# A two-layer spectral filter on one core: the last task's inverse rows are loaded step by step, and its neighbour's held groups go through three pairs of banks

## The reference

```python
f = jnp.fft.fft2(xf, axes=(1, 2), norm='ortho')          # layer 0
Xk = (f.real - f.imag)[:, :, :Wf].reshape(..., 8, 48)[:, lo:hi, :kept]   # kept = 23
o1 = relu(einsum('bhwni,nio->bhwno', Xk, w1[0]) + b1[0])
o2 = einsum('bhwno,nio->bhwno', o1, w2[0]) + b2[0]
x = jnp.fft.ifft2(softshrink(o2, 0.01), s=(H, W), axes=(1, 2), norm='ortho').real + x

xf = jnp.fft.rfft2(x, axes=(1, 2), norm='ortho')         # layer 1, complex weights
o1r, o1i = relu(xr*w1[0] - xi*w1[1] + b1[0]), relu(xi*w1[0] + xr*w1[1] + b1[1])
o2r, o2i = softshrink(o1r*w2[0] - o1i*w2[1] + b2[0]), softshrink(o1i*w2[0] + o1r*w2[1] + b2[1])
y = jnp.fft.irfft2(o2r + 1j*o2i, s=(H, W), axes=(1, 2), norm='ortho') + x
```

## Time and profile before

| what | value |
|---|---|
| median of three runs | 519.68 us |
| the profiled execution: its own time | 517.78 us |
| the profiled execution: its span | 516.0 us |
| mean granted TensorE clock | 0.975 |
| TensorE busy (products) | 479.6 us, 93% |
| VectorE, ScalarE, GpSimd busy | 308.1, 209.8, 172.5 us |
| moved by DMA | 105.25 MB, mean 204 GB/s |

### The profile page before, as it was taken

The page is one execution under the profiler, slowest core; times in us unless marked ns, Lnnn a source line. Parts: engine busy times, 40 slices in busy tenths (PEclk is TensorE's granted clock), DMA queues, the critical chain, the costliest instruction groups (busy, mean ns, idle before and its releaser), DMA issues.

```text
span 516.0 us, 14920 instructions
## 1 busy us (share of the span) xinstructions
PE 479.6 (93%) x6172; PEld 342.5 (66%) x6172; DVE 308.1 (60%) x674; ACT 209.8 (41%) x473; POOL 172.5 (33%) x194
## 2 busy tenths in 40 slices
PE   4679999999999999999999999999999999999763
PEld 1357787777777677767777677767777767886521
DVE  7634456457754677456764677456763577567643
ACT  0015544553355443543354433554345434444201
POOL 9821323123441244223442144312433122322134
PEclk9959999999999999999999999999999999999978
DMA  9998773677899688886989588987989665644498
GB/s 213 265 237 236 213 187 110 145 207 182 252 233 243 165 201 264 218 216 178 267 224 252 152 210 263 228 204 187 256 213 258 169 168 163 148 108 113 121 224 268
DMA packets 77416, 105.25 MB, mean 204 GB/s; under 512 B 7744, under 2 KB 63826, under 8 KB 77350
## 3 DMA queue, kind: packets, MB, share of 16 engines
q1 hardware_dynamic: 57766, 56.74, 41.4%
q0 software_dynamic: 10608, 40.66, 29.8%
q10 hardware_dynamic: 8976, 6.90, 5.7%
HBM read 52.84 MB, written 51.43 MB: 202 GB/s over the span
## 4 chain that ended last, share of the span: by engine, by line
PE 77%; DMA 7%; DVE 5%; POOL 3%; issue 2%; ACT 2%; SPq 1%; ACTq 1%; POOLq 0%
PE ps L702 13%; PE ps L636 13%; PE ps L727 12%; PE ps L689 11%; PE ps L597 10%; PE ps L649 8%; PE ps L714 5%; PE ps L665 4%; PE ps L675 3%; DMA img<-x 2%; DVE img L572 2%; DMA wt<-weights 2%; POOL xs L392 2%; DVE ns L546 2%; ACT p L463 1%
## 5 line engine op out<-in xcount | busy, mean ns | idle before, releaser
L572 DVE TENSOR_TENSOR img<-ps,img 90x768 f32<-90x768 f32 x92 | 82.6, 900 | 19.0 <-PE ps L636 15.5
L392 POOL TENSOR_TENSOR xs<-xs,nt 128x360 f32<-128x360 f32 (+1 forms) x48 | 41.6, 866 | 147.9 <-DVE nt L524 122.5
L636 PE MATMUL ps<-jr,cst 64*90 64x384 f32 (+1 forms) x358 | 80.0, 515 | 6.4 <-DVE img L572 5.7
L597 PE MATMUL ps<-img,cst 128*64 128x384 f32 (+1 forms) x368 | 70.1, 494 | 8.9 <-DMA img<-x 8.0
L401 POOL DMA_DIRECT2D y<-img x42 | 34.7, 826 | 130.7 <-DVE img L572 130.3
L456 ACT ACTIVATE o<-ps,wt 97x180 f32<-97x180 f32 (+1 forms) x96 | 33.9, 406 | 108.7 <-PE ps L689 108.7
L546 DVE SCALAR_TENSOR_TENSOR ns<-p,ps 109x384 f32<-109x384 f32 x96 | 53.1, 553 | 38.2 <-ACT p L463 33.4
L702 PE MATMUL ps<-wt,o 128*64 128x96 f32 x1472 | 74.4, 250 | 0.1
L649 PEld LDWEIGHTS ps<-cst,bt 128*64 128x64 f32 x1472 | 62.5, 140 | 16.9 <-issue 13.9
L702 PEld LDWEIGHTS ps<-wt,o 128*64 128x64 f32 x1472 | 65.4, 138 | 12.5 <-issue 12.5
L689 PE MATMUL ps<-xs,wt 64*97 64x180 f32 (+1 forms) x768 | 68.9, 317 | 3.4 <-POOL xs L392 3.2
(11 more groups left out here) (43 smaller groups left out, 410.9 us busy)
## 6 DMA issues: line engine op xcount, KB each, us to landing
y<-img POOLq DMA_DIRECT2D x35, 540.0 KB, 5.4
img<-x POOLq DMA_DIRECT2D x25, 540.0 KB, 8.6
scr_i<-et SPq DMA_DIRECT2D x48, 270.0 KB, 5.4
scr_f<-fs SPq DMA_DIRECT2D x154, 72.0 KB, 3.4
bt<-scr_f SPq DMA_DIRECT2D x40, 270.0 KB, 5.5
jr<-scr_i SPq DMA_DIRECT2D x48, 216.0 KB, 5.3
img<-x ACTq DMA_DIRECT2D x10, 576.0 KB, 7.8
y<-img SPq DMA_DIRECT2D x11, 270.0 KB, 3.7
```

Of the source, the lines that this page charges most:

```text
L392: nc.gpsimd.tensor_tensor(re, re, nt[s % 2][:, :, 0:kws(s), 0:H], ALU.subtract).then_inc(re_ok, 1)
L572: nc.vector.tensor_tensor(y, p, y, ALU.add).then_inc(i_add, 1)
L597: last = mm(ps[64 * r:64 * r + 64, P3 + g % 2, 0:(b - a) * HC], K["w_fwd"], img[t % IMGS][:, a:b, :].rearrange("p h c -> p (h c)"), start= ...
L636: last = mm(ps[0:W, B0 + r, 0:n], K["w_inv"][64 * r:64 * r + 64, :], set_rows(t, j)[64 * r:64 * r + 64, at, 0:n], start=True, stop=True)
```

## The change

Four things are changed together, all of them at the end of the list.

1. The rows for task 7's inverse W are no longer loaded in five sets after the last step, but step by step in the tile `f0`, which task 0's forward W used: behind the store of step i (from i = 1 on), SP waits until step i - 1 is stored and loads its eight rows for all 12 groups (`last_rows`, three DMAs). The rows of the last step follow in the entry ("last_rows",): SP loads the first half of each group and the last group, ACT's queue the second half. Task 7's first product waits for all of them.
2. The five held groups of task 6, g7 to g11 (`HELD` = 7), go through the pairs P2, P1, P3, P2, P1 (`pair_of`) and not all through P3.
3. POOL's stores of task 6's image rows behind g7, g9 and g11 wait until task 7's rows have all landed.
4. `LAST_POOL` has three groups and not four; ACT copies them in turn into `p1` and a free `et` tile, and issues their stores at its end. VectorE adds the other nine.

The products of task 7 read 48 rows of `f0` and not 64 of `jr` (the 16 others were zero).

```diff
@@ -24,11 +24,12 @@
...
 GROUPS = -(-H // 4)
+HELD = 7
 XCH = 8
...
 WARM = 7
-LAST_POOL = (1, 4, 7, 10)
+LAST_POOL = (1, 4, 7)
 JSETS = [(0, 3), (3, 6), (6, 9), (9, 11), (11, 12)]
...
@@ -149,7 +150,7 @@
...
     order += held
-    order += [("rows", TASKS - 1, j) for j in range(len(JSETS))]
+    order.append(("last_rows",))
     order += [("inv", TASKS - 1, g) for g in range(GROUPS)]
...
@@ -220,7 +221,8 @@
...
         j_ld = [sem(f"j{k}_loaded") for k in range(JR)]
-        j_tail = [sem(f"last_set{j}_loaded") for j in range(JR, len(JSETS))]
+        l_ld = [sem(f"last_rows{k}_loaded") for k in range(2)]
+        y_last_act = sem("y_of_last_task_stored_act")
         i_mm, i_add = sem("inv_product"), sem("inv_added")
...
@@ -241,11 +243,22 @@
...
-        def set_rows(t, j):
-
-            if t == TASKS - 1 and j >= JR:
-                return bt[j - JR][:, 0:(JSETS[j][1] - JSETS[j][0]) * 2 * HC].rearrange("p (g c) -> p g c", c=2 * HC)
-            return jr[bank_of(t, j)[0]]
+        def last_rows(i, r):
+            k0, k1 = 2 * STEP * i, min(2 * STEP * (i + 1), 2 * KWP)
+            rows = scr_i[TASKS - 1].rearrange("k e h c -> (k e) h c")[k0:k1]
+            four = rows[:, 0:H - 1, :].rearrange("q (g r s) c -> q g r (s c)", r=2, s=2)[:, :, r, :]
+            return four, f0[64 * r + k0:64 * r + k1, 0:GROUPS - 1, :], rows[:, H - 1, :], f0[k0:k1, GROUPS - 1, 0:HC]
+        def held_no(t, g):
+            return g - HELD if t == TASKS - 2 else -1
+        def pair_of(t, g):
+            if t == TASKS - 1:
+                return (P0, P1, P2, P3)[g % 4]
+            return (P2, P1, P3)[held_no(t, g) % 3] if held_no(t, g) >= 0 else P3
...
@@ -325,33 +338,41 @@
...
                                  et[s % 2][0:2 * H, :, :]).then_inc(e_st[s % 2], 16)
+                    if t == TASKS - 1 and i > 0:
+                        sp.wait_ge(e_st[(s - 1) % 2], 16 * ((s - 1) // 2 + 1))
+                        for r in range(2):
+                            four, to, one, to_one = last_rows(i - 1, r)
+                            sp.dma_start(to, four).then_inc(l_ld[0], 16)
+                        sp.dma_start(to_one, one).then_inc(l_ld[0], 16)
                 if kind == "rows" or (kind == "inv" and what[0] < TASKS - 1 and what[1] in (2, 5)):
...
                     k, used = bank_of(t, j)
-                    landed = j_tail[j - JR] if t == TASKS - 1 and j >= JR else j_ld[k]
                     if j == 0:
...
                         sp.wait_ge(j_clr, j + 1)
-                    if t == TASKS - 1 and j >= JR:
-                        sp.wait_ge(a_mm, 2 * NT)
-                    elif used:
+                    else:
                         m = t * len(JSETS) + j - JR
...
                     if g0 == GROUPS - 1:
-                        sp.dma_start(set_rows(t, j)[0:2 * KWP, 0, 0:HC], rows[:, 4 * g0, :]).then_inc(landed, 16)
+                        sp.dma_start(jr[k][0:2 * KWP, 0, 0:HC], rows[:, 4 * g0, :]).then_inc(j_ld[k], 16)
                     else:
...
                         for r in range(2):
-                            sp.dma_start(set_rows(t, j)[64 * r:64 * r + 2 * KWP, 0:g1 - g0, :], four[:, :, r, :]).then_inc(landed, 16)
-                if kind == "inv" and what[0] == TASKS - 1:
+                            sp.dma_start(jr[k][64 * r:64 * r + 2 * KWP, 0:g1 - g0, :], four[:, :, r, :]).then_inc(j_ld[k], 16)
+                if kind == "last_rows":
+                    sp.wait_ge(e_st[(NT - 1) % 2], 16 * ((NT - 1) // 2 + 1))
+                    four, to, one, to_one = last_rows(STEPS - 1, 0)
+                    sp.dma_start(to, four).then_inc(l_ld[0], 16)
+                    sp.dma_start(to_one, one).then_inc(l_ld[0], 16)
+                if kind == "inv" and what[0] == TASKS - 1 and what[1] not in LAST_POOL:
                     g, (h0, h1), (b, f) = what[1], hrows(what[1]), divmod(TASKS - 1, HALVES)
...
                     sp.dma_start(out[b, h0:h1, :, f * HC:(f + 1) * HC].rearrange("h w c -> w h c"), img[(TASKS - 1) % IMGS][0:W, h0:h1, :]).then_inc(y_last, 16)
-            sp.wait_ge(y_last, 16 * GROUPS)
+            sp.wait_ge(y_last, 16 * (GROUPS - len(LAST_POOL)))
...
@@ -398,6 +419,10 @@
...
                     pool.wait_ge(i_add, t * GROUPS + g + 1)
+                    if t == TASKS - 2 and g >= HELD:
+                        pool.wait_ge(l_ld[0], 16 * (3 * (STEPS - 1) + 2))
+                        pool.wait_ge(l_ld[1], 16)
                     pool.dma_start(out[b, r0:r1, :, f * HC:(f + 1) * HC].rearrange("h w c -> w h c"), img[k][0:W, r0:r1, :]).then_inc(y_st[k][c], 16)
...
@@ -406,7 +431,8 @@
...
                     y = img[t % IMGS][0:W, h0:h1, :].rearrange("p (r s) c -> p r (s c)", r=2)
-                    nc.gpsimd.tensor_tensor(y, p1[0:W], y, ALU.add).then_inc(i_pool, 1)
+                    p = (p1[0:W], et[NT % 2][0:W].rearrange("p (r s) c -> p r (s c)", r=2))[n % 2]
+                    nc.gpsimd.tensor_tensor(y, p, y, ALU.add).then_inc(i_pool, 1)
                 if kind == "load" and what[0] % STEPS == 3 and what[0] // STEPS >= 2:
...
@@ -467,14 +493,26 @@
...
                     nc.scalar.activation(et[s % 2][0:2 * H, 0::2, :], ps[0:2 * H, P0, 0:2 * HC].rearrange("p (k c) -> p k c", c=HC), ACT.Copy).then_inc(e_act, 1)
+                if kind == "last_rows":
+                    act.wait_ge(e_st[(NT - 1) % 2], 16 * ((NT - 1) // 2 + 1))
+                    four, to, _, _ = last_rows(STEPS - 1, 1)
+                    act.dma_start(to, four).then_inc(l_ld[1], 16)
                 if kind == "inv" and what[0] == TASKS - 1 and what[1] in LAST_POOL:
                     t, g = what
-                    n, B0 = LAST_POOL.index(g), 2 * (g % 4)
+                    n, B0 = LAST_POOL.index(g), pair_of(t, g)
                     act.wait_ge(i_mm, t * GROUPS + g + 1)
                     act.wait_ge(d1_ss, 2 * NT)
-                    if n > 0:
-                        act.wait_ge(i_pool, n)
-                    nc.scalar.activation(p1[0:W], ps[0:W, B0:B0 + 2, 0:2 * HC], ACT.Copy).then_inc(i_act, 1)
+                    act.wait_ge(e_st[NT % 2], 16 * ((NT - 2) // 2 + 1))
+                    if n > 1:
+                        act.wait_ge(i_pool, n - 1)
+                    p = (p1[0:W], et[NT % 2][0:W].rearrange("p (r s) c -> p r (s c)", r=2))[n % 2]
+                    nc.scalar.activation(p, ps[0:W, B0:B0 + 2, 0:2 * HC], ACT.Copy).then_inc(i_act, 1)
+            b, f = divmod(TASKS - 1, HALVES)
+            for n, g in enumerate(LAST_POOL):
+                h0, h1 = hrows(g)
+                act.wait_ge(i_pool, n + 1)
+                act.dma_start(out[b, h0:h1, :, f * HC:(f + 1) * HC].rearrange("h w c -> w h c"), img[(TASKS - 1) % IMGS][0:W, h0:h1, :]).then_inc(y_last_act, 16)
+            act.wait_ge(y_last_act, 16 * len(LAST_POOL))
...
@@ -562,7 +600,7 @@
...
                     h0, h1 = hrows(g)
-                    B0 = P3 if t < TASKS - 1 else 2 * (g % 4)
+                    B0 = pair_of(t, g)
                     dve.wait_ge(i_mm, t * GROUPS + g + 1)
...
@@ -606,34 +644,40 @@
...
                     t, g = what
-                    j = jset[g]
-                    k, _ = bank_of(t, j)
-                    if g == JSETS[j][0]:
-                        if t == TASKS - 1 and j >= JR:
-                            pe.wait_ge(j_tail[j - JR], 16 * set_dmas(j))
-                        else:
-                            pe.wait_ge(j_ld[k], rows_landed(t, j))
-                    at = g - JSETS[j][0]
-                    if t < TASKS - 1:
-                        B0 = P3
-                        vacate(0)
-                        vacate(1)
-                    else:
-                        B0 = 2 * (g % 4)
-                        if g < 4:
-                            pe.wait_ge(i_add, t * GROUPS)
-                            pe.wait_ge(t_add, 2 * NT)
-                            pe.wait_ge(d0_ss, 2 * NT)
+                    B0, n = pair_of(t, g), held_no(t, g)
+                    if t == TASKS - 1:
+                        if g == 0:
+                            pe.wait_ge(l_ld[0], 16 * (3 * (STEPS - 1) + 2))
+                            pe.wait_ge(l_ld[1], 16)
                             pe.wait_ge(e_act, NT)
                             pe.wait_ge(e_dve, NT)
+                        elif g < 4:
+                            users = [m for m in range(HELD, GROUPS) if pair_of(TASKS - 2, m) == B0]
+                            pe.wait_ge(i_add, (TASKS - 2) * GROUPS + (users[-1] if users else HELD - 1) + 1)
                         elif g - 4 in LAST_POOL:
...
                             pe.wait_ge(*last_added(g - 4))
+                    else:
+                        j = jset[g]
+                        k, _ = bank_of(t, j)
+                        if g == JSETS[j][0]:
+                            pe.wait_ge(j_ld[k], rows_landed(t, j))
+                        if n == 0:
+                            pe.wait_ge(d1_ss, 2 * NT)
+                        elif n == 1:
```

(10 more changed lines are left out.)

## The result

The changed kernel takes 522.36 us (median of 20 runs, 519.11 to 527.69), the kernel before beside it 518.74 (20 runs, 516.10 to 520.44). The ratio is 1.0075, 95% interval 1.0054 to 1.0095: slower by 0.75%, where 516.5 us, within 513.0 to 518.8, and a gain had been forecast. The profiled execution took 523.22 us with a span of 521.4, for 517.78 and 516.0 before.

A forecast was written before the change was run, and what follows sets the result against it. The tail was taken as bound by the bytes DMA must move: 496.2 + 15.8 + 0.8 + 0.6 = 513.4, less 0.2, a span of 513.2 against 516.0, gain 2.8 us. Forecast 516.5 us, range 513.0 to 518.8.

The forecast's parts named there:

- the fifteen early loads: Row loads of five steps on SP before 488: put at nothing, or 1.2 us per step without cover.
- the outline of the tail: DMA share nearly nothing for a microsecond or two before 496, then 0.95 or more for 16 us.
- the stores cover the adders and the slow clock: After task 7's products start: adds end by 505.8, well before 511, so half clock and the extra add cost nothing.
- The held groups: Task 6's g7 to g11 in three bank pairs: adds end at 492.9, not 497.6, with VectorE unbroken.
- these 4.7 us: Time taken away ahead of task 7's products by the earlier held adds, if their rows are there.
- The last rows: Last step's row loads before task 7: 3.6 us, between 2.5 and 5.4, so products start at 494.8.
- a sign of being wrong: The prediction is wrong if the last rows' load before task 7 takes over 5 us.
- The rule that the prediction did weigh: Last rows' load from eight partitions uses eight of sixteen engines: rows near 495.5, gain 2.1 us, 10% of 29.
- The late rows as a rival: Last step's load takes 5.4 us, task 7 starts at 496.6, gain only 1.0 us; chance 29%.
- The tail's term: From 496.2 on, 4.56 MB of stores at 289 GB/s take 15.8 us, plus 0.8 of taper.
- the account of before: Stretch 491 to 515 of the kernel before: 24.0 us as 15.8 stores, 0.8 taper, 7.4 loads.
- The rival in which the stores run slower: Tail's 4.56 MB at 212 GB/s take 21.5 us, span 519.1, kernel 3.1 us slower; chance 6%.

The follow-up runs named there:

- e9: e8 with POOL's store behind g7 not held, only those behind g9 and g11; ratio to the kernel before 0.9993.
- e2: The changed kernel without the wait ahead of POOL's held stores of task 6; ratio to the kernel before 1.0036.
- e4: The kernel before with only task 6's held groups moved to three pairs of banks, rows and stores as before; ratio 0.9998.
- e13: e8 with four products of no use instead of eight; ratio to the kernel before 1.0001.
- e3: The changed kernel with the eight rows of each step sent to partitions six apart, stores still held; ratio to the kernel before 1.0018.
- e7: e3 with task 7's twelve stores all on SP's queue, none on ACT's; ratio to the kernel before 1.0017.
- e1: The kernel before with row loads added behind its end; eight-row pairs took 5.73 us to neighbouring partitions, 4.25 to partitions six apart.
- e5: The kernel before with paired loads added behind its end, strided or dense source; eight rows took 6.10 and 6.33 us to neighbours, 4.31 and 4.20 spread.
- e11: The kernel before with the tail's stores added behind its end, nothing else running; all 4.56 MB took 19.6 us.
- e10: e8 with none of POOL's stores of task 6 held; ratio to the kernel before 0.9973 (0.9941 to 1.0004).
- e12: The same kernel as e10 measured once more; ratio to the kernel before 0.9927 (0.9902 to 0.9952).
- e8: e3 with eight products of no use on TensorE ahead of task 7's, to keep its clock up; ratio to the kernel before 0.9994.
- e6: The changed kernel with rows sent to partitions six apart and POOL's stores not held; ratio to the kernel before 0.9995.

## Why the prediction was wrong

**What held.** The step that put the fifteen early loads at nothing: no wait of TensorE for them shows before 488. The 0.66 us upstream can't be put down to them, for the kernels with the same early loads issue the last step's store anywhere from 486.60 (e9) to 490.75 (e2), and e4, without them, at 489.47. Also right were the outline of the tail (the DMA share falls to 0.04, then stays at 0.88 to 0.98 for 16 us, where 0.95 or more had been forecast) and that the stores cover the adders and the slow clock. The last of VectorE's adds ends 11.2 us after task 7's first product (11 forecast) and ten microseconds before the end, and e13 against e3 shows what the clock is worth there. The fourth part of the change, one group more for VectorE and stores on ACT's queue, was not run alone; e7 tests its queue, and only this cover speaks for the rest of it giving and costing nothing.

**The held groups.** "Four adds at 0.96 and one of 0.35 end at 492.9", with VectorE unbroken. It was 494.3. The products of g7 and g8 run on from 488.15, but those of g9 to g11 (the ten at 491.29) start only when the add of g8 has ended at 491.15: TensorE idles 1.37 us and VectorE 1.07. The banks of g9 don't ask for that, as it goes through P3, which g6 used last; but its code takes the old wait (`vacate`), which by then stands for the add of g8. The order of instructions shows a wait for `inv_added` on g9, and the prediction passed it over. It cost nothing, since the rows came at 499.98. The prediction counted these 4.7 us on the condition that the rows are there; e4 shows that in the kernel before the rows would have ended the wait at nearly the same time.

**The last rows: the step that failed.** "I take 3.6 us, a third of the way up", between 2.5 and 5.4. It was 7.2, outside both bounds, since both were loads that go to 48 partitions each, and over the 5 us that the prediction itself had named as a sign of being wrong. The 3.6 us between are more than the whole gain of 2.8 that it forecast. Eight neighbouring partitions are another case: 5.7 to 6.3 us for the pair with nothing beside it, 4.2 to 4.3 spread (e1, e5). Here the fifth step's load, issued at 489.61 to the same kind of target, is ahead of it on the same queue. SP's queue moves 123 packets from 492.8 to 495, while ACT's load, issued at 492.79, has its first packets only after 495. How the 7.2 us divide between the two steps' loads was not measured apart. With the spread both end in 4.6 us after the first issue (e3), and the ratio of the kernel goes from 1.0075 to 1.0018: this step is worth most of the loss, and what keeps the gain away even then lies in the tail. The same effect fits the 0.9 us of the last step's store: 3.53 and 3.47 us where the fifth step's load beside it goes to neighbours (the changed kernel, e2), 2.62 to 2.64 where it is spread (e3, e13) or absent (e4).

The Trainium skill ("SBUF — State Buffer", "Door 1: The DMA port swizzle") says that DMA bandwidth depends on how many of sixteen ports the partitions of a transfer reach, with 27.2 GB/s for each. By its table partitions 40 to 47 reach two ports and 104 to 111 two others, so the pair could have 109 GB/s; an estimate from that page would be 2.5 us for its 0.27 MB, where the changed kernel moved 68 to 83 GB/s from 492 to 498. The direction agrees, with the 1.5 to 2.1 us that spreading saves the pair (e1, e5). By the same table sixteen partitions three apart reach all clusters and sixteen neighbours half of them, and the gain there is 0.5 us at most (5.83 against 6.35 in e5, 4.23 against 4.28 in e1), so the rule does not cover all that was measured. The rule that the prediction did weigh from the Trainium skill ("DMA: Bandwidth & Descriptors", "Why a DMA increments its semaphore by 16 and not by 1"), that eight rows use eight engines, fits the share of about one half; but the share is one half for spread rows as well (0.52 in e3), so it cannot tell the two apart.

**The late rows as a rival** had the right place and the wrong size: its dearest case was 5.4 us for a gain of 1.0. With 7.2 the same sum gives a span of 516.8, a loss of 0.8. It set some five microseconds of emptied engines against seven saved. The runs show seven against four: 1.82 MB put off and 1.03 MB fewer to move, each at 260 GB/s. (The two last steps' rows are 0.55 MB by the shapes and not 0.57, which changes nothing.)

**The tail's term was mis-sized**: the 4.56 MB of stores at 289 GB/s, 15.8 us, were read off the four cuts in which stores ran alone with the engines full. From the first held store to the end the sum has 18.4 us (1.4 to the first data, 15.8, 0.8 and 0.6, less 0.2), and it took 20.7; e11 measures 19.6 for the same bytes alone, and e7 and e13 leave little to the queue and the clock. The rest, 0.6 to 1.1 us, is open. Its cuts run at 221 to 290 GB/s, and the last two at 248 and 208. In the account of before the same mistake was hidden, as what stores were charged too little for, loads were charged too much for: from the first store's issue at 490.08 to the end it is 25.9 us, which less the 19.6 leaves 6.3 for the loads and not 7.4. POOL's first issue, 0.7 us after the products' start rather than with it, completes the 3.0 us. The rival in which the stores run slower had this mechanism at 6%; what was found, 235 GB/s from 502 to the end, lies between its 212 and the forecast's 289.

**The hold itself.** Without it the changed kernel gains (1.0036 for 1.0075), and the spread one with busy TensorE gains too (0.9973 in e10 and 0.9927 in e12, for 0.9994 in e8 and 1.0001 in e13). Without the hold the clock may matter as well, since task 7's stores can then go out only as its adds end: from e6 to e12 the ratio falls from 0.9995 to 0.9927, but the interval of e10, the same kernel, overlaps that of e6. So this is argued from the thin cuts of e6 and not shown. How the gain divides between clock and scatter is left open by the width of the intervals.

## What to carry to other kernels

Where DMA bounds the end of a kernel, holding ready stores to make room for a small load must be paid from the load's own duration, and that has to be measured for its very partitions; price the bytes of a tail by its mean rate with start and taper, not by its full cuts. When a load is cut into steps of a few rows, let each step go to partitions spread over the whole range; that paid for eight rows here, and hardly for sixteen. Two things that end together (here the held groups and the rows) give nothing when one of them is shortened.
